# A graph network layer on one core: GpSimd waits for its last gathers to land, three times a group

## What is computed

```
def _L0_gnn_ref(input, adj, weight, bias):
    h = input @ weight
    out = jnp.maximum(adj @ h + bias, 0.0)
    return _graph_pool(out, adj)      # row i: max over all j with adj[i, j] != 0 of out[j]
h = jnp.maximum(_layernorm(x, axis=-1), 0.0)
x = x + _L0_gnn_ref(h, adj, L0_gnn_weight, L0_gnn_bias)
```

## Time and profile before

| what | value |
|---|---|
| runs of the kernel before | 1907.07, 1901.81, 1894.20 us; median 1901.81 us |
| profiled execution, its own time | 1901.04 us |
| its span, first to last instruction | 1899.3 us |
| outside the span | 1.7 us |
| mean granted TensorE clock | 0.909 |
| TensorE matmul / VectorE / ScalarE / GpSimd busy | 84% / 66% / 37% / 30% |
| pool stage with its gathers, 357 to 825 us | 468 us; TensorE busy 293, GpSimd busy 220 |

### The profile page before, as it was taken

How to read it: one execution, slowest core, us unless ns; L and a number is a source line. 1 busy time by engine, 2 the same in 40 slices (tenths; PEclk the granted TensorE clock), 3 DMA queues, 4 the chain that set the end, 5 groups by cost and what they waited for, 6 DMA issues and landing times.

```text
span 1899.3 us, 32560 instructions
## 1 busy us (share of the span) xinstructions
PE 1592.9 (84%) x9151; PEld 929.2 (49%) x9161; DVE 1255.6 (66%) x3487; ACT 704.4 (37%) x1113; POOL 570.5 (30%) x813
## 2 busy tenths in 40 slices
PE   4999999666565776499997999789999999866897
PEld 4777777323222332156664666578644444333453
DVE  6899999646454666374665666723299999942343
ACT  3444444234333444222333222456555555510000
POOL 5233333454455444500011000223200000055663
PEclk8999999777777877699999999889999999987998
DMA  7687886322222222222221322234200000033442
GB/s 256 232 295 292 292 293 250 92 82 62 79 73 69 76 79 60 65 69 94 97 91 52 115 89 88 82 106 127 84 1 6 6 9 8 6 101 102 130 139 70
DMA packets 127159, 205.04 MB, mean 108 GB/s; under 512 B 11440, under 2 KB 95536, under 8 KB 118912
## 3 DMA queue, kind: packets, MB, share of 16 engines
q1 hardware_dynamic: 102592, 172.58, 26.9%
q0 software_dynamic: 11840, 25.52, 5.0%
q10 hardware_dynamic: 12672, 6.29, 1.1%
HBM read 178.13 MB, written 26.21 MB: 108 GB/s over the span
## 4 chain that ended last, share of the span: by engine, by line
PE 58%; DVE 15%; issue 14%; another core or an unknown queue 8%; ACT 2%; POOL 1%; DVEq 1%; DMA 0%; ACTq 0%; POOLq 0%; SPq 0%
PE bank L680 24%; PE bank L605 7%; PE bank L566 7%; PE bank L750 6%; DVE partsA L2112 5%; PE bank L817 3%; PE bank L594 3%; DVE cand L1586 3%; PE bank L571 2%; PE bank L542 2%; PE bank L529 2%; PE bank L818 1%; ACT first L918 1%; DVE partsA L2128 1%
## 5 line engine op out<-in xcount | busy, mean ns | idle before, releaser
L680 PE MATMUL bank<-partsB,panel 128*128 128x387 bf16 (+1 forms) x2048 | 366.2, 337 | 55.2 <-issue 37.6
L680 PEld LDWEIGHTS bank<-partsB,panel 128*128 128x128 fp8e4 x2048 | 203.3, 100 | 213.9 <-issue 70.7
L1726 DVE TENSOR_TENSOR gath<-gath,bank 128x512 f32<-128x512 f32 x240 | 162.0, 682 | 202.2 <-remote 122.9
L817 PE MATMUL bank<-wide,partsA 128*128 128x512 f32 x512 | 263.3, 596 | 7.0 <-ACT rows L1111 4.9
L918 ACT ACTIVATE first<-bank 128x512 fp8e4<-128x512 f32 x256 | 150.6, 597 | 297.5 <-remote 142.1
L594 PE MATMUL bank<-panel,tri 128*128 128x512 fp8e4 x256 | 109.5, 429 | 168.6 <-ACT first L918 141.2
L605 PE MATMUL bank<-first,partsB 128*128 128x512 fp8e4 x768 | 240.9, 429 | 5.4 <-DVE gath L1722 5.4
L1586 DVE MAX8 cand<-bank 128x8 f32<-128x128 f32 x1024 | 216.7, 284 | 10.4 <-PE bank L571 7.8
L566 PE MATMUL bank<-partsA,panel 128*128 128x387 bf16 x1024 | 212.1, 329 | 7.5 <-DVE cand L1586 6.1
L872 ACT ACTIVATE panel<-bank 128x1024 fp8e4<-128x1024 bf16 x128 | 130.9, 1024 | 147.8 <-PE bank L542 147.8
L1307 POOL DMA_INDIRECT gath<-pool_features,idx_now x160 | 159.8, 999 | 80.4 <-issue 46.7
(11 more groups left out here) (290 smaller groups left out, 2153.3 us busy)
## 6 DMA issues: line engine op xcount, KB each, us to landing
rows<-in_adj SPq DMA_DIRECT2D x64, 1024.0 KB, 7.1
panel<-adjT_panels SPq DMA_DIRECT2D x96, 512.0 KB
panel<-adjT_panels SPq DMA_DIRECT2D x128, 256.0 KB, 2.8
adjT_panels<-panel SPq DMA_DIRECT2D x32, 512.0 KB, 3.0
gath<-pool_features,idx_now POOLq DMA_INDIRECT x160
overflow_maxima<-wide POOLq DMA_DIRECT2D x1, 2048.0 KB, 21.2
pool_features<-gsc ACTq DMA_DIRECT2D x8, 256.0 KB, 2.3
rows<-overflow_maxima SPq DMA_DIRECT2D x8, 256.0 KB
```

What stands on the lines that cost most here:

```text
L680: i = pe.matmul(bank[q][:, 0:3 * w], panel[:, q, j, :], of_block if w < FE else parts_of[u][:, j, :], start=(j == 0), stop=(j == NT - 1))
L817: pe.matmul(o[:, :], zs[:, q % 2, :], zT[:, c * 512:(c + 1) * 512], start=True, stop=False)
L1726: dve.tensor_tensor(running[:, j % 2, :], running[:, j % 2, :], pool_bank[j % 4][:, :], ALU.max).then_inc(s_fp_used, 1)
```

## The change

A helper waits until all five gathers of one tile of this group have landed. GpSimd calls it before it issues the gathers of q = 1 (for those of q = 0), before the overflow gathers (for those of q = 1) and before the gathers of q = 3 (for those of q = 2). Nothing else is altered; the same DMAs are issued in the same order.

```diff
+            def rows_landed(g, q):
+
+                pool.wait_ge(s_gath[q], 16 * MAIN * (g + 1))
+
             def gathers(g, q):
                 t = g * G + q
                 pool.wait_ge(s_idx, t + 1)
                 pool.wait_ge(s_gath_used, t + 1)
+                if q in (1, 3):
+                    rows_landed(g, q - 1)
                 pool.sem_inc(waited["pool"], 1)
                 for k in range(MAIN):
...
                 for q in range(G):
                     gathers(g, q)
                     if q == 1:
+                        rows_landed(g, q)
                         overflow_gathers(g)
                     if q == 3:
                         store_overflow(g)
```

## The result

The changed kernel takes **1822.07 us** (median of 4, 1818.22 to 1829.73) where the kernel before takes 1899.55 (median of 4, 1894.20 to 1907.07): a ratio of 0.959, 95% interval 0.954 to 0.964. Its profiled execution took 1825.57 us, 75.5 less than the 1901.04 of before. On two other chips parts of the change cost time; the experiments come to that.

A forecast was written before the change was run, and what follows sets the result against it. Unbroken GpSimd gather runs delaying TensorE's signals were taken to bound the pool stage. Per group 23.8 - 11.9 - 3 - 1 - 0.7 = 7.2 us, 50 in seven, plus 4 in group 0: 1901.0 less 54 is 1847 us, range 1790 to 1908.

The forecast's parts named there:

- What bounds: Pool stage: TensorE's results are reported late while GpSimd issues runs of gathers; 166 us lost over groups 1 to 7.
- Cost of a wait, 1.35 us: First wait delays q = 1's gathers: landing 2.3 plus issue 0.3 less normal spacing 1.25; the pause becomes 2.6 us.
- too short: Rival: 2.6 us pauses clear nothing, each wait lengthens the stall, 22 us, 1923; most of slower's chance of 0.19.
- Third wait hidden: Wait before q = 3 is over before reached, as indices come 4.96 us late; if early, it costs 1.35 us.
- The cover: GpSimd's slack, 4.96 us before q = 3 and 16.72 before the store, absorbs the waits; otherwise 22 us in eight groups.
- Terms of the sum: Pool stage losses per group after the change: q = 0 alone 3, q = 1 alone 1.0, q = 3 1.0 instead of 0.3.
- overflow and q = 2: These gathers stay one run, a window of 14.4 us at 0.82 lost per us: 11.9 us lost a group.
- the long stall: Today's TensorE stall beside a group's unbroken gather run of 24.9 us: 23.8 us lost a group, 0.82 per us of window.
- The sum: Pool stage gain: 7.2 us a group, 50 us in seven, plus 4 us in group 0, 54 together.
- The signs to look for: Profile after: "remote" waits 246 to about 130 us, TensorE over 80% busy after q = 0 and q = 1, stores near 48 apart.
- No change: Rival: something else in the pool stage makes the stall, and the waits vanish in GpSimd's slack: 1901 us, chance 0.14.
- Much faster, 1767: Rival: each short run is free and the long run's first eight gathers cost nothing: 134 us gained, chance 0.14.

The follow-up runs named there:

- the 1680 chip: Chip on which the kernel before takes 1679.74 us; a second such chip takes 1681.67. The changed kernel itself was never run on one.
- the memsets: Kernel before with GpSimd memsets at the three places instead of waits: three each 1852.03 us (0.970), five each 1822.82 (0.957); on the 1680 chip three took 1715.24.
- the 1900 chip: Chip on which the kernel before takes 1905.28 and 1902.79 us in two sets; the changed kernel took 1816.16 and 1821.48 there.

## Why the prediction was right, and where not

The forecast's mechanism, sign and range held on the chip whose trace it was read from: 1822 for 1847, in the range and at the edge of the forecast's own (1822 to 1880). Step by step:

- **What bounds.** Right there: pauses alone, made of memsets, bring all of the gain. That "remote" came from runs of gathers and grew with their length was right too. The forecast said nothing of other chips, and there the first step fails: in the kernels traced on the other two no wait for "remote" stands, and in those with gathers by index GpSimd's chain is the bound.
- **Cost of a wait, 1.35 us: too low.** Measured 2.13 in group 3 (511.35 to 514.73 less 1.25). Two terms of the sum were off. The 2.3 us of rows 12 aren't the gathers': the view takes the whole tile, and on the page before only the writes into it have a time:

```profile
gath<-pool_features,idx_now POOLq DMA_INDIRECT x160
...
pool_features<-gsc ACTq DMA_DIRECT2D x8, 256.0 KB, 2.3
```

The gathers take 2.5, by the row of the 1680 chip above; on this chip the copy behind the second wait begins 2.78 us after the last issue (519.72 to 522.50), so they take no longer here. The larger error is the 0.3 us to issue, which is the gap between gathers back to back. After a wait it is 0.8: when the second wait is over GpSimd copies the indices (522.50, 0.19 us), and its first overflow gather begins at 523.50, 0.81 us after the copy's end. 2.5 + 0.8 is 3.3 of the 3.38 us. The error helped the forecast's cause: the break is 3.4 us, not 2.6, and by the memsets 2.6 would have left the kernel at 1852. The rival "too short" put its threshold at about 3 us with a cost of 22 us below it; at 2.58 us there was a gain of 53, so the rival's price was wrong. Its worry was half right, as the shorter break does lose two fifths of the gain.
- **Third wait hidden: no.** With VectorE no longer late, its indices are there early (`stage` at 529.30, the last q = 2 gather at 534.76), so this wait costs 2.13 us as well. The text had named that condition.
- **The cover held.** GpSimd's idling before the store went from 16.72 to 4.05 and 8.11 us: spent, but not used up. In the kernels with gathers by index that were traced on the 1680 chips it isn't there (0.30), and that is the price that the text gave for lost cover, mis-sized: it said 22 us in eight groups (two waits at 1.35), and two cost 40.7.
- **Terms of the sum**, a group: q = 0 alone 3 (measured 2.5), q = 1 alone 1.0 (1.6), q = 3 with the cold clock 1.0 + 3.1 (4.5), overflow and q = 2 **11.9 (7.9)**. The last is the term that was mis-sized. It took the rate of the long stall, 0.82, for a window of 14.4 us; but that rate is that of a run of twenty, most of it past its first few microseconds. TensorE in fact worked until 530.7, 7.2 us after the run's first gather, then did little until 538:

```profile
529.80:538.00 8.20, 2.76 (x9) 0.70 (x6) 1.79 (x6) 0.84 (x2) 4.68 (x5) 0.70 0.27 76
```

- **The sum.** 7.2 us a group forecast, 9.5 by the table and 9.8 by the stores; group 0: 4 forecast, 5.0 measured. The stores' 68.8 us against 50, group 0's 1.0 and 1.6 elsewhere make the 21 us by which the profiled execution is faster than forecast. The long run's term, 4.0 a group or 28 us in seven, is more than all of it; part of that is given back, since the loss before was 26.0 a group by the table where the forecast's terms had 27.2 (23.8 + 0.3 + 3.1).
- **The signs to look for.** "Remote" 246 to about 130: 115. Store to store near 48: 47.46. TensorE over 80% busy after q = 0 and q = 1: over groups 1 to 7 it is busy for 68% of the stretch of the store and q = 0 and for 87% of that of q = 1, so this held for one of the two. In group 3 it is 73% in both, and each short run still ends in a stall, of 2.6 and 1.9 us.
- **No change, by the page "SBUF — State Buffer", section "Who interferes with whom", of the Trainium skill** (TensorE and ScalarE wait for no one, a DMA doesn't contend with an engine). The 1680 chip's trace agrees: 0.15 us from matmul to reader beside the gathers. The 1900 chip's doesn't: 3.4 to 7.1 us. And the advice of the Trainium skill's page "DMA: Bandwidth & Descriptors", section "Rules for kernel authors", to wait late, which the forecast set aside, is what the 1680 chip bears out: 40.7 us for two early waits.
- **Much faster, 1767:** not seen; short runs aren't free (2.5 and 1.6 a group).

What stays open: what holds TensorE's news back on one chip and not on others, whether the descriptors by index or any GpSimd DMA do it, whether a break must be as long as a landing, and what a fourth break would bring there.

## What to carry to other kernels

Where an engine waits for "remote" while its producer has long finished, look at what GpSimd issues at that time, and test it with a pause of plain filler before reasoning on: the pause alone showed that the unbroken runs of gathers were the cause and that 3.5 us bring more than 2.6. Look up whose landing time a view gives, add to it what the engine needs from the end of a wait to its next DMA (0.8 us here, not the 0.3 between two in a row), and ask what slack the wait is paid from: the same three waits gained 4% where that slack was 17 us a group and cost by their parts an estimated 3% where it was 0.3. And look at the kernel before on more than one chip before tuning to a stall of this kind, since here one chip took 220 us longer than two others, on which no such stall was seen.

## What was not expected of the hardware

- One kernel takes 1897 to 1920 us on one chip and, but for the one execution named above, 1679 to 1685 on two others. In the traces the difference is in the pool stage, 468 us against 312 with one wait in it, and in the last stage, where the two traces of the kernel before have 70 and 84 us of "remote" waits at L1520.
- The lateness has a shape: cheap for the first 3 to 6 us of a run of gathers, then 22 `select` matmuls in 49 us, and largely gone after a break of 3.4 or 3.5 us in the issuing, filled with a wait or with memsets.
- Tripling the increments of TensorE's own counter left the time as it was (1909.29 against 1905.28).
- The traces of the 1900 chip also lack most records of landings. Of the 640 updates by which the gathers of q = 0 report, that of the kernel before holds 95 and that of the changed kernel 192, the one with two waits on the 1680 chip 631. All waits for them were met, so the updates came; why their records are missing there stays open.
- On the 1680 chip the wait after q = 0 was longer than elsewhere, 3.90 us of idling against 2.44, so the landing took 1.5 us more right behind the store; no run follows this up.
